# The edges' keys lose their group offset on POOL, and DVE compares with one scalar

## The reference, cut to what matters

```
src = jnp.concatenate([edge_index[0], loops])
dst = jnp.concatenate([edge_index[1], loops])
deg = jax.ops.segment_sum(jnp.ones_like(dst, jnp.float32), dst, num_segments=n)
dinv = jnp.where(deg > 0, jax.lax.rsqrt(deg), 0.0)
norm = dinv[src] * dinv[dst]
...
msg = norm[:, None] * hw[src]
return jax.ops.segment_sum(msg, dst, num_segments=n) + b
```

## Time and profile before

| | |
|---|---|
| median of 3 runs | 4912.1 us |
| profiled execution, first to last instruction | 5413.3 us |
| its build stage, 51 to 655 us | 604 us |
| DVE busy in the build | 545.5 us |
| PE busy in the build | 491.3 us |
| ACT busy in the build | 387.3 us |
| POOL busy in the build | 0 us |
| runs of four chunks / groups | 276 / 125 |

### The profile page before, as it was taken

How to read it: one execution, slowest core, us unless ns; L and a number is a source line. 1 busy time by engine, 2 the same in 40 slices (tenths; PEclk the granted TensorE clock), 3 DMA queues, 4 the chain that set the end, 5 groups by cost and what they waited for, 6 DMA issues and landing times. The chain is left out here.

```text
span 5413.3 us, 92595 instructions
## 1 busy us (share of the span) xinstructions
PE 4136.6 (76%) x24432; PEld 3019.5 (56%) x24433; DVE 2377.6 (44%) x6354; ACT 1465.5 (27%) x3183; POOL 551.5 (10%) x662
## 2 busy tenths in 40 slices
PE   5888666996998976527164592497988889979999
PEld 2444344665866953316152361396953389947776
DVE  8988788885012115505032112503035543633333
ACT  3566615774011021101011131200001122423333
POOL 1000000000000000171716301000011100000000
PEclk9999957887989998658587796699989955989999
DMA  2111202222421510111101212342520000010000
GB/s 95 53 72 76 100 17 74 89 85 93 170 87 61 196 47 3 22 29 38 12 20 27 28 42 82 129 178 98 190 89 0 0 1 0 0 23 12 12 12 24
DMA packets 134062, 322.83 MB, mean 60 GB/s; under 512 B 47723, under 2 KB 85135, under 8 KB 119466
## 3 DMA queue, kind: packets, MB, share of 16 engines
q1 hardware_dynamic: 114612, 297.00, 15.8%
q0 software_dynamic: 14000, 10.47, 1.8%
q10 hardware_dynamic: 5354, 14.21, 0.7%
HBM read 246.14 MB, written 76.96 MB: 60 GB/s over the span
## 5 line engine op out<-in xcount | busy, mean ns | idle before, releaser
L537 PE MATMUL ps<-hot_key,hot_src 128*126 128x512 bf16 (+1 forms) x2208 | 432.1, 314 | 40.6 <-DVE hot_key L502 10.3
L502 DVE TENSOR_SCALAR hot_key<-col_iota,edge_key,neg_group 128x625 bf16<-128x625 int16 x1104 | 461.3, 440 | 0.0
L2164 POOL DMA_INDIRECT fetched<-node_table,src_idx x384 | 387.8, 1010 | 124.5 <-issue 124.5
L1321 PE MATMUL ps<-gnn_u_thirds,near 125*128 125x256 bf16 x3000 | 337.3, 275 | 22.3 <-issue 22.3
L537 PEld LDWEIGHTS ps<-hot_key,hot_src 128*126 128x126 bf16 x2208 | 213.7, 136 | 250.4 <-DVE hot_key L502 171.2
L1321 PEld LDWEIGHTS ps<-gnn_u_thirds,near 125*128 125x128 bf16 x3000 | 331.0, 141 | 27.2 <-issue 24.3
L2269 PE MATMUL ps<-xnT,ew 128*128 (+2 forms) x640 | 201.3, 470 | 168.9 <-issue 94.0
L2988 PEld LDWEIGHTS ps<-scores_kv,phi_cols 128*125 128x125 f32 x1800 | 290.3, 246 | 0.5 <-issue 0.5
L2988 PE MATMUL ps<-scores_kv,phi_cols 128*125 128x33 f32 (+1 forms) x1800 | 286.2, 313 | 0.1
L2269 PEld LDWEIGHTS ps<-xnT,ew 128*128 128x128 f32 x640 | 128.3, 207 | 236.0 <-issue 119.0
L2303 PE MATMUL ps<-table_thirds,src_hot 125*128 125x168 bf16 x1536 | 134.4, 245 | 159.5 <-issue 155.7
(11 more groups left out here) (535 smaller groups left out, 7245.5 us busy)
## 6 DMA issues: line engine op xcount, KB each, us to landing
near<-adjacency SPq DMA_DIRECT2D x80, 1562.5 KB, 6.6
adjacency<-counts SPq DMA_DIRECT2D x125, 312.5 KB, 2.2
own_in<-own_rows SPq DMA_DIRECT2D x34, 512.0 KB, 4.0
expert_rows<-rows_y SPq DMA_DIRECT2D x100, 125.0 KB
pair_in<-high_rows SPq DMA_DIRECT2D x34, 256.0 KB, 4.9
pair_in<-low_rows SPq DMA_DIRECT2D x34, 256.0 KB, 5.7
agg0a_adj<-adjacency SPq DMA_DIRECT2D x5, 1562.5 KB
spare<-adjacency SPq DMA_DIRECT2D x5, 1562.5 KB, 9.7
```

What stands on the lines that cost most here:

```text
L502: nc.vector.tensor_scalar(hot_key[:, j, :], col_iota[:], edge_key[:, ds(chunk, 1)], neg_group[:, ds(group, 1)], ALU.subtract, ALU.is_equal ...
L537: last = nc.tensor.matmul(sums[:, b:e], hot_src[:, j, :], hot_key[:, j, b:e], start=False, stop=True, skip_group_check=True)
L1321: last = nc.tensor.matmul(ps[:, j, 0:width], lead_tiles[BUF[j]][:, k, :], parts.thirds[:, k, i, :], start=(k == 0 and i == 0), stop=(k == ...
L2164: pool.indirect_dma_start(out=fetched[:, q, j, :], out_offset=None, in_=node_table, in_offset=bass.IndirectOffsetOnAxis(ap=src_idx[:, q, j ...
```

## The change

POOL gets a loop over the groups and their runs. For each run it adds the group's column of `neg_group` to the four keys of the run, 128 x 4 numbers, and writes them to `group_key`, which has a part for each of the five groups of a tile. Line 502 of before (519 now) then reads its key from `group_key`, and has one scalar in place of two. Two semaphores tie the engines together: DVE waits before a run's first key block until POOL has made the run's keys (`keys_made`), and POOL waits before a group until DVE is done with the group that used the same part five groups earlier (`keys_used`). DVE raises `keys_used` at each group's end, behind a wait by `alone` for its own first key block of that group.

```diff
+                group_key = q("group_key", [128, TG, CHUNKS_PAD])
...
-                @block.gpsimd
-                def _(pool):
-                    pool.wait_ge(most_ready, 2)
-                    nc.gpsimd.partition_all_reduce(deg_all[:], deg_most[:], 128, RMAX).then_inc(most_reduced, 1)
...
+                @block.gpsimd
+                def _(pool):
+                    with pool.Fori(0, T) as tile:
+                        for k in range(TG):
+                            group = tile * TG + k
+                            first, runs, _, _ = ranges_of(mybir.EngineType.Pool, group)
+                            alone(pool, keys_used, group + 1)
+                            with pool.Fori(0, runs) as i:
+                                chunk = nc.s_assert_within(
+                                    first + i * RUN, 0, CHUNKS_PAD - RUN, skip_runtime_bounds_check_because=(
+                                        "a group's runs end with its last chunk, or a run after the first"))
+                                nc.gpsimd.tensor_tensor(group_key[:, k, ds(chunk, RUN)], edge_key[:, ds(chunk, RUN)],
+                                                        neg_group[:, ds(group, 1)].to_broadcast([128, RUN]), ALU.add).then_inc(keys_made, 1)
+                    pool.wait_ge(most_ready, 2)
+                    nc.gpsimd.partition_all_reduce(deg_all[:], deg_most[:], 128, RMAX).then_inc(most_reduced, 1)
...
                 @block.vector
                 def _(dve):
+                    dve.sem_inc(keys_used, TG - 1)
...
                                     if j < RUN - 1:
                                         nc.vector.tensor_scalar(hot_src[:, j, 0:P], col_iota[:, 0:P],
                                                                 src_low[:, ds(chunk, 1)], None, ALU.is_equal)
-                                    nc.vector.tensor_scalar(hot_key[:, j, :], col_iota[:], edge_key[:, ds(chunk, 1)],
-                                                            neg_group[:, ds(group, 1)], ALU.subtract,
-                                                            ALU.is_equal).then_inc(hot_ready, 1)
+                                    if j == 0:
+                                        dve.wait_ge(keys_made, n + 1)
+                                    nc.vector.tensor_scalar(hot_key[:, j, :], col_iota[:], group_key[:, k, ds(chunk, 1)],
+                                                            None, ALU.is_equal).then_inc(hot_ready, 1)
+                            alone(dve, hot_ready, before * RUN + 1)
+                            dve.sem_inc(keys_used, 1)
```

More of the change, by code:

```diff
@@ L452, in graph_kernel @@
                 hot_ready = sem("hot_ready")
+                keys_made = sem("group_keys_made")
+                keys_used = sem("group_keys_used")
                 squared = sem("src_squared")
```

## The result

The changed kernel takes 4966.9 us, median of four runs (4964.55 to 4968.51), where the kernel before took 4907.84 and 4912.1: a ratio of 1.0099, 95% interval [1.0056, 1.0142]. That is +57 us; the forecast was +28, with a range that ends at 4990. On another chip, where both kernels take some 410 us longer, the changed kernel took 5382.0 against 5323.3: 1.0109 [1.0091, 1.0127].

The account below looks back on a forecast made before the run. In the 604 us build, DVE's datapath bounds long groups, PE's loop two-run groups, DVE's sequencer short ones. Changed, the sequencer needs 276 x 1.89 + 125 x 0.80 + 10 = 632 us: +28, 4912 to 4940 us; range 4880 to 4990.

Parts of the forecast that it names:

- The saved scalar: DVE's key blocks in the build: 0.057 us less for each of 1104, 63 us of DVE's time.
- the first rival: Build: added DVE issue is hidden and the PE loop decides, -29 us, 4883 us; chance 0.20 for hidden at least in part.
- the PE loop: Build, chain through PE and DVE's blocks once per group: a two-run group falls from 4.39 to 4.16 us.
- What the sequencer costs: DVE's instruction issue in the build: 0.11 us more a run, 0.35 a group, 632 us in all.
- The first group's 18 runs: Build's longest group, where DVE's datapath decides: 1.90 us a run before, forecast to stay as it was.
- a group's end: DVE's sequencer between groups of the build: 0.45 us beyond another run before, 0.80 with the added instructions.
- the long loads: DVE sequencer's load at a group's end, at times 0.735 instead of 0.349 us: allowed once a tile, 10 us.
- the second (the scalar frees nothing): Build: DVE's datapath stays at 1.90 us a run, PE loop at 4.39, about 4945 us; chance 0.08.
- A difference in this stage should carry over to the unprofiled runs one to one: The build: PE's clock is already whole there in the profile, so the 604 us is the base of the sum.
- something outside the build: Stages other than the build: something there moves the time by more than 98 us; chance 0.02.
- POOL holds DVE: Build: each POOL add stalls DVE, 0.39 us a run, 109 us on top, 5049 us; chance 0.12.

Follow-up runs that it names:

- e3: The kernel before with one scalar in the key block and nothing else, the group's offset left out: 5299.8 us, ratio 0.9947.
- e6: The changed kernel with keys laid out by run and no wait or semaphore at a group's end: 5321.7 to 5332.1 us, ratio 0.9997.
- e2: The changed kernel with both scalars kept in the key block, POOL's keys waited for but unused: 5387.2 us, ratio 1.0124.
- e4: The changed kernel with one small POOL add ahead of the build: 5391.9 us, ratio 1.0129.
- f1: The kernel before with 10 more DVE memsets ahead of the build, which ends 33.8 us later: 5356.5 to 5367.6 us, ratio 1.0077.
- f2: The kernel before with 7 more DVE memsets ahead of the build, which ends 23.4 us later: 5350.2 us, ratio 1.0055.
- e5: The kernel before with 12 more DVE memsets ahead of the build, which ends 43 us later: 5360.7 to 5369.6 us, ratio 1.0083.
- f3: The changed kernel with 4 more DVE memsets ahead of the build: 5367.1 us, ratio 1.0083.
- g: Four kernels (before, changed, changed with early POOL add, keys by run with one wait per tile) plus 42 PE transposes: ratios 1.0057, 1.0113, 1.0107, 0.9936.
- h: The kernel before and the changed kernel, each with 68 PE transposes at the head of the last stage: ratios 1.0059 and 1.0113.
- e1: The kernel before, unchanged, profiled a second time: ratio 1.0005, profiled span 5323.9 us.
- h2: The changed kernel with 68 PE transposes at the last stage's head: 5346.5 us (one run) or 5389.9 to 5397.9 (four), ratio 1.0113.
- h1: The kernel before with 68 PE transposes at the last stage's head: 5326.7 to 5332.2 us or 5366.3 to 5373.3, ratio 1.0059.
- e8: The kernel before with POOL's 276 adds running beside it, neither waited for nor used: ratio 0.9996, build 602.4 us against 602.6.
- g1: The kernel before with 42 PE transposes at the last stage's head: 4915.5, 4948.5 and 4951.7 us, ratio 1.0057.

## Why the prediction was wrong in size, step by step

**The saved scalar: right.** 381 ns and starts 0.29 to 0.30 apart were forecast and measured. That the scalar was worth 27 us by itself (e3), as the first rival had it, shows the PE loop of 4.16 us too: e6 has 4.18.

**What the sequencer costs: right in the sum, not in its parts.** e6 splits it. From one scalar alone to keys by run the build grows from 575.3 to 591.2, 0.058 us for each of 276 runs (0.11 forecast). From there to the changed kernel it grows by 37.6, 0.30 for each of 125 groups (0.35 forecast). With the 27.3 saved, 15.9 + 37.6 - 27.3 = 26.2 us, against 28. Part of the run's price stays hidden in the PE loop in e6, so the 0.058 is not a price of the instructions.

The first group's 18 runs show a run without a group's end: it takes 1.81 us in the changed kernel, 1.73 in e3 and 1.90 before, where the forecast had 1.89 and let the first group stay as it was. So a run was priced 0.08 too dear, 22 us over 276 runs. A group's end was too cheap: if all the rest is theirs, (628.8 - 276 x 1.81) / 125 = 1.03 us for each, against 0.80 and 0.08 for the long loads. (Those 10 us were read too high as well: only nine of the 125 loads before are long, 2.6 us together.) The two errors nearly cancel, and the closeness of 26 to 28 is in part luck. By size of group, the 79 of two runs give 16 us of the 26 (4.44 to 4.64 each) and the 24 of one run 8 (2.48 to 2.83). e2 confirms the bound from the other side. So the first rival (hidden) is out, and of the second (the scalar frees nothing) only its time was near.

**"It may be up to four groups ahead, so DVE meets the keys ready except at the start, where its memsets of some 3 us cover POOL's first run": failed, +8 us.** That POOL keeps ahead held: one wait in the whole build. But I had priced POOL's start like any other add, and its first add behind the all-reduces comes 12.0 us after the queue has reached it. e4 takes this away with one earlier add, and the build starts 7.6 us sooner. What in the switch takes the 12.0 us stays open: the earlier add comes 6.9 us behind its own queue record in e4.

**"A difference in this stage should carry over to the unprofiled runs one to one", and nothing behind the build changes: failed, +26 us.** The prediction gave 0.02 to something outside the build, and this is the larger part. 4.5 us come back before the last stage, and that is mostly the clock too. Between 2229 and 2256 us the kernel before has a granted 0.52, where the changed one, 32 us later, has 0.83 and needs 4.8 us less for the same matmuls (before, then changed):

```profile
2229.40:2256.00 26.60, 21.90 (x52) 8.96 (x52) 3.96 (x22) 3.38 (x8) 0.00 (x0) 0.52 0.00 0
```

```profile
2261.90:2284.00 22.10, 16.65 (x52) 6.62 (x52) 4.27 (x23) 3.38 (x8) 0.00 (x0) 0.83 0.00 0
```

Then 30.3 us arise where PE's clock stays low for 99 us in place of 38. Over the profiles the last stage's length follows that stretch: 979 us with 14, 983 to 990 with 38 (eight profiles), 1017 to 1022 with 96 to 99 (five), 1027 to 1037 with 116 to 143 (four), 1074 and 1077 with 232. Going from 38 to 99 costs 30.3 us for 61.5, 0.5 us for each microsecond, as half the clock should on an engine that works: PE stands for 10.1 us of the 38 and for 8.6 of the 99.

What sets the stretch's length is open, but the profiles show what it goes with: the moment of the fall. Counted from the start of the transposes of line 2819, the clock falls between 0.13 us before and 0.09 us after it in all eight profiles with 38 us, 2.67 us after it in the two with 232, 2.98 in the one with 143 (e4), and 3.05 to 3.08 in the three with 99. So a few tenths of a microsecond in that moment go with 130 us of stretch. No run set this moment on purpose, so it is a link and not a shown cause. A delay of the build (f1, f2, e5), the build's kind of work (f3), and the standstill's length between 5 and 10 us (g and h) do not decide the length by themselves, and one kernel can have more than one: the kernel before has 38 us in e1 and 232 in its first profile. It isn't mere chance either: all eight timed runs of the changed kernel on two chips lie together, within 4 and 7 us, and both profiles show the 99 us. So as timed, the change costs 57 us. With a last stage of the same kind it costs less: 17 and 24 us by h2 against h1, and by f3 against e1 some 31, its 43 less the 12 us by which it was delayed. The forecast's +28 is about that, and wrong for what is measured. As one kernel can have a short or a long last stage, no single number is the price of the change.

**POOL holds DVE: rightly not the forecast.** e8 shows no loss at all. The range reached up to 4990 for this rival's sake, and that is what kept the result inside it, for another reason: this is luck.

## What to carry to other kernels

Count an engine's sequencer like its datapath: where small instructions follow closely, one more wait and increment for each group can cost as much as the datapath saves, and the remedy is a layout that needs no hand-over (by run here) or one wait for many groups. Before work moves to an engine that stood still, look at what it ran last: here POOL's first add behind its all-reduces came 12 us late, and an add of one column earlier in the program hid that. And a kernel's difference should be read stage by stage: when a stage that the edit doesn't touch changes by tens of microseconds, look at the granted clock there before crediting or blaming the edit.

## What was not expected of the hardware

- The same stage ran at the lower clock level for 38, 99, 143 or 232 us around the same standstill of 10.1 us, and took 983 to 1077 us. The lengths recur over kernels and chips: 38 us in eight profiles, 99 in three, 232 in two. Each goes with a moment of the fall that is the same to 0.03 us, but for 0.2 us among the eight.
- In the eight profiles with 38 us the clock fell ahead of the long standstill, behind two short ones of PE of 1.8 and 2.2 us. The profiles with longer stretches have short ones of 1.8 or 1.9 and 2.2 us there too, and their clock was still whole behind these.
- An add of 128 x 4 numbers costs POOL 0.199 us typically, 57.8 us for 276, and 85.8 us where nothing makes them wait; neither slows DVE's blocks of 625 columns.
- Chips differ by 8% on this kernel (4911 against 5321 to 5328 us) with the same times in the build. At the first `fetched` they are still level (2282.8 us in g1, 2284.6 in e1), at the last `fetched` they stand at 2814.3 and 3038.4, and at the first add to `v_sum` at 3601.0 and 4016.1.
